# Six stages of a gated cross-attention and mixture-of-experts kernel: one block of programs in place of six

## The reference

```python
x = x + tanh(g_xattn[0]) * L0_xattn(layernorm(x), ctx, ctx, ...)   # one head of 256
x = x + tanh(g_ffn[0])   * L0_ffn(layernorm(x), ...)               # 8 experts, top 2 of each row
x = x + tanh(g_xattn[1]) * L1_xattn(layernorm(x), ctx, ...)        # 16 heads of 64
x = x + tanh(g_ffn[1])   * L1_ffn(layernorm(x), ...)               # 8 experts, each takes its best 256 rows
...
# L0_ffn: every row goes through its two best experts
probs = softmax(xf @ gate_w.T); weights, idx = top_k(probs, 2); weights /= weights.sum()
out_all = (silu(xf @ w1.T) * (xf @ w3.T)) @ w2.T                    # hidden size 512
# L1_ffn: every expert picks 256 rows of each batch
gating, idx = top_k(softmax(x @ gate_w.T).T, 256)
h = silu(x[idx] @ w_gate.T) * (x[idx] @ w_up.T)                     # hidden size 1024
out = zeros.at[idx].add(gating * (h @ w_down.T))
```

## Time and profile before

| | us |
|---|---|
| median of 3 runs | 1564.45 |
| lowest and highest run | 1563.13, 1567.84 |
| the profiled execution | 1565.53 |
| its span, first to last instruction | 1563.8 |
| mean granted clock of TensorE | 0.882 of full speed |

### The profile page before, as it was taken

How to read it: one execution, slowest core, us unless ns; L and a number is a source line. 1 busy time by engine, 2 the same in 40 slices (tenths; PEclk the granted TensorE clock), 3 DMA queues, 4 the chain that set the end, 5 groups by cost and what they waited for, 6 DMA issues and landing times. The chain is left out here.

```text
span 1563.8 us, 30547 instructions
## 1 busy us (share of the span) xinstructions
PE 1317.8 (84%) x9756; PEld 983.7 (63%) x9757; DVE 975.7 (62%) x2085; ACT 654.9 (42%) x1979; POOL 652.6 (42%) x651
## 2 busy tenths in 40 slices
PE   6787409899999969799999970079999999999995
PEld 2566408799999945588888860035556655666554
DVE  1887605655555546588888869855666566655650
ACT  1876303433233325588888842023333333323220
POOL 1367744666666651154454433031422243223313
PEclk8655559999999976899999995589999999999998
DMA  4544213643333341001011021032333333232212
GB/s 130 202 143 144 80 25 72 128 62 63 65 64 61 63 101 35 1 22 34 27 34 34 28 68 54 0 136 85 84 75 87 89 77 84 67 108 31 38 14 27
DMA packets 75077, 107.14 MB, mean 69 GB/s; under 512 B 20278, under 2 KB 66876, under 8 KB 71932
## 3 DMA queue, kind: packets, MB, share of 16 engines
q0 software_dynamic: 29312, 37.31, 14.9%
q1 hardware_dynamic: 44700, 68.62, 13.4%
q10 hardware_dynamic: 992, 0.27, 0.1%
HBM read 69.65 MB, written 36.52 MB: 68 GB/s over the span
## 5 line engine op out<-in xcount | busy, mean ns | idle before, releaser
L1699 POOL DMA_INDIRECT out_x<-yo,gidx x64 | 101.5, 1586 | 338.8 <-ACT yo L1779 324.2
L1810 DVE SCALAR_TENSOR_TENSOR hid<-psU,sil 128x512 f32<-128x512 f32 x128 | 88.5, 691 | 188.5 <-ACT sil L1768 186.1
L906 POOL DMA_INDIRECT x_rows<-yo,tabs x78 | 125.1, 1604 | 109.0 <-ACT yo L973 91.4
L1768 ACT ACTIVATE sil<-psG 128x512 f32<-128x512 f32 x128 | 76.4, 597 | 205.3 <-PE psU L115 197.4
L1351 ACT ACTIVATE pr<-psS,mx 128x77 f32<-128x77 f32 x512 | 158.3, 343 | 6.2 <-DVE mx L1482 4.4
L113 PE MATMUL psYb<-W1h,hh 128*128 128x256 f16 x512 | 139.6, 273 | 1.8 <-ACT yo L1779 1.8
L115 PE MATMUL psYb<-W1h,hl 128*128 128x256 f16 x512 | 139.6, 273 | 0.0
L114 PE MATMUL psYb<-W1l,hh 128*128 128x256 f16 x512 | 139.6, 273 | 0.0
L1001 DVE SCALAR_TENSOR_TENSOR hid<-psU,sil 128x512 f32<-128x512 f32 x78 | 53.8, 690 | 128.2 <-ACT sil L964 128.2
L1351 ACT ACTIVATION_READ_ACCUMULATOR pr<-psS,mx 128x1 f32 x512 | 115.1, 225 | 0.0
L113 PE MATMUL psG<-gxh,W1h 128*128 128x512 f16 x256 | 97.9, 382 | 6.4 <-DVE gxl L1801 5.4
(11 more groups left out here) (316 smaller groups left out, 4143.9 us busy)
## 6 DMA issues: line engine op xcount, KB each, us to landing
w1s<-in_w SPq DMA_DIRECT2D x16, 1536.0 KB, 6.4
stage<-in_w SPq DMA_DIRECT2D x8, 1536.0 KB
X<-in_x SPq DMA_DIRECT2D x8, 512.0 KB, 8.9
n_rows<-xc SPq DMA_DIRECT2D x8, 512.0 KB
x_rows<-X SPq DMA_DIRECT2D x8, 512.0 KB
X<-x_rows SPq DMA_DIRECT2D x8, 512.0 KB
out_x<-X SPq DMA_DIRECT2D x32, 128.0 KB, 1.7
n_rows<-xn SPq DMA_DIRECT2D x32, 128.0 KB, 1.8
```

Of the source, the lines that this page charges most:

```text
L906: pool.indirect_dma_start(x1_rows[:, :], bass.IndirectOffsetOnAxis(tabs[:, j, n, 0:1], 0), yo[:, par, n, :], None, compute_op=ALU.add).the ...
L1699: pool.indirect_dma_start(out_rows[:, :], bass.IndirectOffsetOnAxis(gidx[:, half, col:col + 1], 0), yo1[:, j % 2, n, :], None, compute_op= ...
L1768: act.activation(sil1[:, f % 2, :], psG1[f % 2][:], ACT.Silu, scale=1.0 / (SX * SW)).then_inc(d_sil, 1)
L1810: dve.scalar_tensor_tensor(hid1[:, f % 2, :], psU1[f % 2][:], SH / (SX * SW), sil1[:, f % 2, :], ALU.mult, ALU.mult).then_inc(d_hid, 1)
```

## The change

The programs of each stage become functions (`attn0_sync`, `ffn0_gpsimd`, ...), and a single block at the end calls them one after the other on each engine. The drains and meetings between the stages are gone. In their place each program waits for what it needs of the stage before, with explicit waits. `yo`, `tabs` and `bo4` get places of their own in SBUF, since they are still read while stage 3 begins, and `bo4` becomes one row that is repeated by the DMA instead of four copies. Some instructions get a semaphore to raise (`d_firstl`, an eighth step of `c_aff`, `u_n1`). No arithmetic changes. With the changed indentation left out, the diff is:

```diff
-        with nc.Block() as block:
-            @block.sync
-            def _(sp):
+        def attn0_sync(sp):
...
     in_order(pool, steps, POOL0_ORDER, NG, straight=True)
-    for n in range(2):
-        pool.wait_ge(s_sct[n], 16 * T)
...
-tabs = sb("tabs", [P, NB0, NB, 2], I32, e0)
-yo = sb("yo", [P, 2, NB, D], F32, e0)
-bo4 = sb("bo4", [1, B, 2, D], F16, r1, "right")
+yo = sb("yo", [P, 2, NB, D], F32, r1, "right")
+tabs = sb("tabs", [P, NB0, NB, 2], I32, r1, "right")
+bo4 = sb("bo4", [1, 1, 2, D], F16, r1, "right")
...
 # ffn0_sync
+    sp.wait_ge(s_blk, 15)
+    for n in range(2):
+        sp.wait_ge(s_sct[n], 16 * T)
     sp.dma_start(gts1[:], a["gate1"]).then_inc(b_w1, 16)
...
 # ffn0_gpsimd
-    pool.wait_ge(b_out[0], 16 * NB * ((NB0 + 1) // 2))
-    pool.wait_ge(b_out[1], 16 * NB * (NB0 // 2))
 # ffn0_vector
+    dve.wait_ge(s_wp, NG)
...
 # prep_sync
+    sp.wait_ge(b_out[0], 16 * NB * ((NB0 + 1) // 2))
+    sp.wait_ge(b_out[1], 16 * NB * (NB0 // 2))
     for g in range(NG):
         sp.dma_start(X[:, GT * g:GT * g + GT, :], x1v[:, GT * g:GT * g + GT, :]).then_inc(u_x, 16)
     sp.wait_ge(u_b, 2)
     sp.wait_ge(u_nl, 5 * B)
-    sp.dma_start(N1[...], bo4[:].rearrange("p b a d -> p b (a d)")).then_inc(u_x, 16)
-    sp.wait_ge(u_x, 16 * (NG + 1))
+    sp.dma_start(N1[...], bo4[:].rearrange(...).to_broadcast([1, B, 2 * D])).then_inc(u_n1, 16)
 # prep_gpsimd
+    pool.wait_ge(b_y, NB0)
 # prep_tensor
+    pe.wait_ge(b_w1h, len(PIECES))
+    pe.wait_ge(b_w1l, len(PIECES))
     for m in range(HP):
+        if m == 2:
+            pe.wait_ge(b_yo, NB0)
 # prep_vector
+    dve.wait_ge(b_y, NB0)
...
 # attn1_sync
-    for n in range(2):
-        sp.wait_ge(c_out[n], 16 * T)
 # attn1_gpsimd
+    pool.wait_ge(u_nl, 5 * B)
 # attn1_tensor
+    pe.wait_ge(u_ml, 4 * KD * B)
+    pe.wait_ge(u_nl, 5 * B)
+    pe.wait_ge(u_n1, 16)
 # attn1_vector
+    dve.wait_ge(u_x, 16 * NG)
...
 # topk_sync, topk_gpsimd, topk_tensor
+    sp.wait_ge(c_av[2], T)
+    pool.wait_ge(c_aff, 8)
+    pe.wait_ge(c_aff, 8)
...
 # ffn1_sync (before the third load), ffn1_gpsimd, ffn1_tensor
+    sp.wait_ge(d_firstl, 2)
+    pool.wait_ge(k_dve, KSTEPS)
+    for n in range(2):
+        pool.wait_ge(c_out[n], 16 * T)
+    pe.wait_ge(d_firstl, 2)
```

More of the change, by code:

```diff
@@ new lines, in weights_low, with top_logits @@
+            def weights_low(g, par):
+                dve.wait_ge(s_wh, g + 1)
+                dve.tensor_tensor(Wl[:, bass.ds(g * W0E, HW)], stage[:, par, 0:HW], Wh[:, bass.ds(g * W0E, HW)],
+                                  ALU.subtract).then_inc(s_wl, 1)
+            def top_logits(g, par):
+                dve.wait_ge(s_lg, g + 1)
+                for i in range(GT):
+                    last = dve.max(top[:, GT * g + i, :], psL[:, i * E:(i + 1) * E])
+                last.then_inc(s_cho, 1)
@@ new lines, in ffn0_scalar, with rows_high, silu, run @@
+        def ffn0_scalar(act):
+            def rows_high(j, par):
+                act.wait_ge(b_xt, j + 1)
+                wait(act, b_g[1], j - 1)
+                act.activation(bxh[:, par, :, :], psX[par][:, :, :], ACT.Copy, scale=SX).then_inc(b_xh, 1)
+            def silu(half):
+                def run(j, par):
+                    act.wait_ge(b_g[half], j + 1)
+                    act.activation(sil[:, half, :, :], psG[half][:, :, :], ACT.Silu, scale=1.0 / (SX * SW))\
+                       .then_inc(b_sil[half], 1)
+                return run
+            def results(j, par):
+                act.wait_ge(b_y, j + 1)
+                if not isinstance(j, int) or j >= 2:
+                    act.wait_ge(b_out[par], 16 * NB * (j // 2))
+                for n in range(NB):
+                    last = act.activation(yo[:, par, n, :], psY[par][:, n, :], ACT.Copy,
+                                          scale=tabsf[:, bass.ds(j * (2 * NB) + (2 * n + 1), 1)])
+                last.then_inc(b_yo, 1)
+            def high_piece(j, par):
+                i = piece_of(j)
+                if i is None:
+                    return
+                name, _, _, scale = PIECES[i]
+                act.wait_ge(b_w1, 32 + 16 * sum(len(regions(n)) for n in range(i + 1)))
+                for rows, c0_, c1_ in regions(i):
+                    ins = act.activation(split1[name][0][0:rows, c0_:c1_], raw1[0:rows, c0_:c1_], ACT.Copy, scale=scale)
+                ins.then_inc(b_w1h, 1)
+            pipeline(act, NB0, PEEL, [(2, silu(0)), (1, rows_high), (2, silu(1)), (3, results), (1, high_piece)])
```

2107 lines of the change are left out of this document (1039 added, 1068 removed).

## The result

The changed kernel takes 1536.13 us (median of 4 executions, 1535.4 to 1537.9) against 1563.79 us (also 4 executions, one more than stood behind the 1564.45 of the prediction). The ratio is 0.9817, its 95% interval 0.9803 to 0.983. Forecast were 1536.5 us and a ratio of 1536.5 / 1564.45 = 0.982. The profiled execution took 1536.31 us, its span 1534.2: 29.6 us less than the 1563.8 of before.

What follows compares the result with a forecast made beforehand. TensorE was busy 84% of the span, so the change touches only five seams: 5.7 + 19.4 + 2.3 + 0.2 + 0.3 = 27.9 us, taking the median from 1564.45 to 1536.5 us; range 1529.5 to 1545.5.

Steps and rivals of the forecast that it cites:

- Seam 1: attn0 to ffn0: SyncE waits for the scatters itself and loads without GpSimd's 5.29 us drain ahead; gain 5.7 us.
- The rule that speaks against seam 1: attn0 to ffn0: if GpSimd's drain were a constant of some 12 ns, the gain would be some 0.4 us.
- Seam 2: ffn0 to prep: three chains start earlier, GpSimd's memsets end last, products start at 587.8 instead of 607.21; gain 19.4 us.
- These start at the lower clock and gain nothing further: Products of prep: TensorE idles 11 us ahead of them, so they start at the lower clock as before, no further gain.
- Seam 3: prep to attn1: VectorE goes on without waiting for the bias row's DMA and the meeting; gain 2.3 us.
- Seam 4: VectorE's last affinities to TensorE's start: of 0.30 us only a semaphore's way stays; gain 0.2 us.
- Seam 5: Last indices to ffn1's first gather: most is the way from wait to indirect DMA, which stays; gain 0.3 us.
- The drain as work that delays what follows even where no drain stands: Rival at seams 1 and 2: GpSimd needs the drain's time anyway, gather and memsets come as late as before; 1546.8, chance 8%.
- no other engine drains so long: Point given for the rival that GpSimd's drains of 5.29 and 2.50 us are work, not waiting; that rival's chance 8%.
- The clock in the projections: Rival at seam 2: TensorE's clock falls to 1.2 GHz in the projections, products start at 593.7, not 587.8; 1542.4, chance 8%.
- VectorE's memsets beside GpSimd's adds: Rival at the end of ffn0: VectorE's memsets delay GpSimd's last adds and its memsets up to 3.1 us; 1539.6, chance 6%.
- Slower indirect DMAs without drains: Rival in ffn0's pipeline: without drains each indirect DMA takes longer; at 0.75 us each 47 us more, 1583, chance 2%.

Runs made afterwards that it cites:

- run with drains alone: Changed kernel, no meetings, with three drains of GpSimd: two behind the landing of attn0's last scatter, one behind ffn0's last adds; 1542.74 us.
- two runs that relieved it in different ways: Changed kernel with GpSimd's eight memsets as 32-bit zeros, 1534.46 us; changed kernel with the same 16-bit memsets ahead of its last pair of adds, 1532.2 us.
- after once more: The changed kernel as it is, nothing edited, in another execution beside later runs; median of that series 1538.19 us.
- run with the clock held up: Changed kernel with 88 more products on TensorE, into unread PSUM columns, between its last projection and the products of prep; 1535.96 us.
- after: The changed kernel in its first profiled execution, 1536.31 us; median of its runs 1536.13 us against 1563.79 before.

## Why the prediction was right, step by step

- **Seam 1, 5.7 us forecast, 5.8 measured.** The amount is right, the reading of it was half of the story: the meeting by itself is worth 3.0 us, the landing wait that stood on GpSimd ahead of its drain 2.8. The prediction took drain and landing for two things in a row by nature; they are so only if GpSimd is made to wait first. The change removed both, so the sum did not suffer.
- **The rule that speaks against seam 1.** The earlier trace rows stood against the constant of some 12 ns that the Trainium skill gives for the drains of the runtime's own code (VectorE: DVE Perf Modes, section The DRAIN you can't avoid). The run with drains alone settled that this one is not of that kind: 5.292 us without any meeting. Only the second of two in a row, 0.034 us, comes near that figure.
- **Seam 2, 19.4 forecast, 19.8 measured.** The two longest chains ran as worked out: VectorE done 21.9 us behind the last product (forecast 584.4 - 562.98 = 21.4), GpSimd's memsets 24.3 us behind it (24.7), products 24.4 us (24.8). The projections ran at 1.00, as forecast, but TensorE was done 16.1 us behind and not 14, and then idle for 8.4 us and not 11. The 13 us were those of a TensorE that nothing holds, while the same paragraph has VectorE take 17 us for the eight pairs. It was not on the path. That GpSimd bounds the products is shown by two runs that relieved it in different ways and both came to 22.0 us, with VectorE as the next.
- **"These start at the lower clock and gain nothing further"** was right. The products took 1.0 us more than before in the profiled execution, with the clock at 0.50 for longer, but 0.2 less in after once more. The whole effect of the low clock is 1.4 to 2.6 us, by the run with the clock held up.
- **Seam 3, 2.3 forecast, 2.4 measured**; the meeting is 1.7 of it, the wait for the bias row 0.8. TensorE's clock was down there again, as before.
- **Seam 4, 0.2 and 0.2:** TensorE starts 0.69 us behind the start of the last affinities (904.83 to 905.52), 0.93 before. **Seam 5, 0.3 forecast, 1.0 measured:** mis-sized. I put most of the 1.26 us between indices and gather down to the way from a wait to an indirect DMA. That way is 0.29 us; the rest was the meeting.
- **The sum.** The seams gave 5.8 + 19.8 + 2.4 + 0.2 + 1.0 = 29.2 us against 27.9. That the mechanism was right is shown by the seams. That the median met the forecast within 0.4 us is luck: the same program once more had 1538.19, and attn0 alone spreads over 5 us. In the profiled pair attn0 was 1.4 us shorter and prep 1.0 longer, which nearly cancels; in after once more ffn0 is 1.6 longer and attn1 and ffn1 are 2.0 and 1.7 shorter than before. The 4 us to either side were needed, and for attn0 more than for the stages that I named.
- **The rivals.** The drain as work that delays what follows even where no drain stands: GpSimd's memset followed its add after 0.05 us. That no other engine drains so long was too much said: at the end of stage 1 TensorE's drain took 3.9 us, and at the end of stage 5 ScalarE's took 2.8, both more than the 2.50 of the earlier trace rows. The clock in the projections: 1.00. VectorE's memsets beside GpSimd's adds: in after VectorE's first memset of V2 ran from 556.51 to 558.27 beside an add (from 556.13) that took 1.54 us like the others. The fear came from the earlier trace rows, and these rows are no single case: all six scatters of attn0 that started while such a subtraction ran took 1.7 to 2.1 us, before and after, and those that started ahead of one and ran into it took 0.97 or 0.98. Slower indirect DMAs without drains: ffn0 is as long as before (338.0 and 338.0; 339.6 once more, far from the 47 us of that rival).

## What to carry to other kernels

A meeting of engines costs what its slowest arrival costs: read each engine's drain in the rows of the block's end, and ask what stood ahead of it. Here GpSimd's drain behind indirect DMAs ended 4.1 to 6.7 us behind the last of them, and 4.8 to 9.6 us with a landing wait ahead of it; a single wait on the engine that needs the data replaced both. Price every seam by its own chain, then name the next bound. Here this was GpSimd's memsets: zeros as 32-bit words, in time that GpSimd had idle, with finer waits behind them and two small loads moved, gave some 7 us more.

And where times spread by 3 us from execution to execution, judge an edit of 2 us by the distance between two rows that enclose it, not by the median.

## What the runs showed of the hardware that I had not expected

- A drain of GpSimd that begins behind landed scatters takes 5.29 us (5.289, 5.289, 5.292 in three kernels); one that is queued behind the last scatter with no wait between ends 6.7 us after it, where landing (4.1 us) and drain one after the other took 9.6; a second drain takes 0.034 us.
- The first indirect DMA behind the two drains started 0.8 us after them, though SyncE had issued the table's load at 219.7, 3.6 us before the drains ended (in after the gather came 2.1 us behind that load); behind another indirect DMA it is 0.3 us.
- A memset on GpSimd goes by elements: 64x2464 of 16 bits 2.15 us, the same bytes as 64x1232 of 32 bits 1.12 us.
- attn0, the same code in all fourteen traces, took between 208.9 and 214.0 us. The 384 matmuls of prep's products took 34.75 us at a granted clock of 1.00 (TensorE kept busy up to their start) and 36.2 to 37.5 at 0.96 to 0.92 (TensorE idle ahead of them).
- A scatter that GpSimd started while VectorE's 1.73 us subtraction of two tiles ran took 1.7 to 2.1 us instead of 0.97.
